# A graph network kernel: a third pair of banks for the first pass's sums, and one-hots by one wide comparison

## The reference

```python
# layer 0: attention by a scalar score per edge
logits = leaky(h_trans[src] @ a_src + h_trans[dst] @ a_dst); exp_l = exp(logits)
alpha = exp_l / (segment_sum(exp_l, dst)[dst] + 1e-09)
h_neigh = segment_sum(alpha * (x @ W1.T + b)[src], dst)
# layer 1: four heads, weights from Q[dst] * K[src]; agg = segment_sum(weighted V[src], dst)
# layer 2: e = silu(silu(cat(h[row], h[col]) @ We1 + be1) @ We2 + be2); agg = segment_sum(e, row)   # the edge MLP
# layer 3: two graph convolutions, out = segment_sum(h[row] * norm, col)
```

## Time and profile before

| | |
|---|---|
| median of 3 runs | 6950.0 us (6945.59 to 6977.82) |
| span of the profiled execution | 5685.5 us, 82572 instructions |
| around the span (median less span) | 1264.5 us |
| busy in the span: POOL | 3958.0 us, 70% |
| DVE | 3263.6 us, 57% |
| PE | 3113.8 us, 55% |
| ACT | 1491.5 us, 26% |

### The profile page before, as it was taken

How to read it: one execution, slowest core, us unless ns; L and a number is a source line. 1 busy time by engine, 2 the same in 40 slices (tenths; PEclk the granted TensorE clock), 3 DMA queues, 4 the chain that set the end, 5 groups by cost and what they waited for, 6 DMA issues and landing times. The chain is left out here.

```text
span 5685.5 us, 82572 instructions
## 1 busy us (share of the span) xinstructions
PE 3113.8 (55%) x17051; PEld 2734.5 (48%) x17052; DVE 3263.6 (57%) x12090; ACT 1491.5 (26%) x5626; POOL 3958.0 (70%) x4054
## 2 busy tenths in 40 slices
PE   4444444356666666778898988433333443333333
PEld 3333333345555555657777776333333343333332
DVE  6888887676787787744444444433444443344445
ACT  2333333345555555532222223100000000000001
POOL 3777777736777777367777772677777757777774
PEclk7555555568888777865555556666666666666666
DMA  5111112214444444222121110111111121111112
GB/s 123 52 52 52 52 52 56 49 52 131 132 132 131 130 131 131 70 54 56 52 56 51 53 52 21 56 52 51 51 51 51 51 61 52 51 51 51 51 51 57
DMA packets 222234, 385.68 MB, mean 68 GB/s; under 512 B 85452, under 2 KB 121882, under 8 KB 221998
## 3 DMA queue, kind: packets, MB, share of 16 engines
q0 software_dynamic: 142944, 296.35, 19.0%
q1 hardware_dynamic: 79054, 86.72, 5.0%
HBM read 356.23 MB, written 26.56 MB: 67 GB/s over the span
## 5 line engine op out<-in xcount | busy, mean ns | idle before, releaser
L2246 POOL DMA_INDIRECT arena<-table_gcn,idx_now x1568 | 1532.2, 977 | 642.9 <-issue 422.1
L2296 PE MATMUL pair<-arena,hotf 128*128 x3328 | 726.6, 408 | 1224.7 <-POOLq L1819 1199.3
L2296 PEld LDWEIGHTS pair<-arena,hotf 128*128 128x128 f32 x3328 | 691.2, 317 | 1256.1 <-issue 1255.8
L664 POOL DMA_INDIRECT arena<-table_attention,idx_now x832 | 825.7, 992 | 272.7 <-issue 197.2
L664 POOL DMA_INDIRECT arena<-table_key_value,idx_now x832 | 789.2, 949 | 275.9 <-issue 221.1
L1852 POOL DMA_INDIRECT arena<-table_edge_mlp,idx_now x784 | 768.1, 980 | 261.2 <-issue 212.4
L2323 DVE TENSOR_TENSOR acc<-acc,pair 128x1024 f32 x208 | 253.9, 1221 | 1133.9 <-PE pair L2299 1133.9
L1069 PE MATMUL pair<-wide,hotf 128*128 128x130 f32 x1664 | 431.0, 439 | 653.3 <-ACT wide L1033 653.3
L1069 PEld LDWEIGHTS pair<-wide,hotf 128*128 128x128 f32 x1664 | 369.0, 326 | 718.5 <-ACT wide L1033 718.5
L2256 ACT COPY idx_now<-src_t 128x8 int32 (+1 forms) x204 | 39.3, 197 | 1815.2 <-PE pair L2299 1803.2
L1406 PE MATMUL pair<-wide,hotf 128*128 128x132 f32 x1664 | 314.1, 347 | 232.9 <-DVE acc L1436 232.8
(11 more groups left out here) (371 smaller groups left out, 5709.7 us busy)
## 6 DMA issues: line engine op xcount, KB each, us to landing
key<-rel_dram SPq DMA_DIRECT2D x104, 256.0 KB, 3.4
arena<-rel_dram SPq DMA_DIRECT2D x52, 512.0 KB, 3.7
arena<-table_gcn,idx_now POOLq DMA_INDIRECT x1568, 2.5
arena<-table_attention,idx_now POOLq DMA_INDIRECT x832
arena<-table_key_value,idx_now POOLq DMA_INDIRECT x832
arena<-table_edge_mlp,idx_now POOLq DMA_INDIRECT x784, 2.4
table_attention<-arena SPq DMA_DIRECT2D x13, 512.0 KB, 3.0
table_gcn<-acc SPq DMA_DIRECT2D x26, 256.0 KB, 2.3
```

The source lines that it names most:

```text
L664: q_.indirect_dma_start(ring[:, slot, 0:width], None, table, bass.IndirectOffsetOnAxis(ap=idx_now[:, slot:slot + 1].bitcast(U32), axis=0)) ...
L2246: q_.indirect_dma_start(conv_ring[:, slot * D:(slot + 1) * D], None, table, bass.IndirectOffsetOnAxis(ap=idx_now[:, slot:slot + 1].bitcast ...
L2296: t_.matmul(window[:, bass.ds(offset * D, D)], hot8[:, g % 2, u, :], conv_ring[:, bass.ds(slot * D, D)], start=False, stop=False)
```

## The change

The first pass gets a third pair of banks for its sums (`l0_bank`: pairs 0, 1 and 3 of PSUM in turn, one bank of a pair for each two steps). Additions are made three groups later instead of two. PE waits for the group three before. A product of the sort that used pair 3 goes to pair 2. The four one-hots of a group are made by one `tensor_tensor` of 128x512 (`hots`, which exists already), and in the edge MLP the eight of a group by one of 128x1024; both compare `iota`, repeated, with `rel_now`, repeated. `rows_of` gets a second register and an operation that bounds the loaded value from below.

```diff
--- before.py
+++ after.py
@@ -735,6 +735,10 @@
         rel_out = junk[:, 1, :].bitcast(BF16)[:, 0:COLS]
         turned, late, decoded = [], {}, []
         LOOKED_UP = (ITERS - 3) * RING
+
+        def l0_bank(k, u):
+
+            return pair[(0, 1, 3)[k % 3]][:, u // 2 * 512 + u % 2 * AW:u // 2 * 512 + u % 2 * AW + D + 2]
 
         def unrolled(step):
 
@@ -865,7 +869,7 @@
                     dve.wait_ge(sort_lastB, 1)
                     ch(v.scalar_tensor_tensor(out=key[:, :].rearrange("q (b p) -> q b p", **by_block),
                                               in0=iota[:, :].unsqueeze(1).to_broadcast([P, SORT // P, P]), scalar=float(SORT // P),
-                                              in1=pair[3][:, :].rearrange("q (b p) -> q b p", **by_block), op0=ALU.mult, op1=ALU.add))
+                                              in1=pair[2][:, :].rearrange("q (b p) -> q b p", **by_block), op0=ALU.mult, op1=ALU.add))
                     counts, e, node, base = (tiny[:, n, :] for n in range(4))
                     for b in range(SB):
                         yield
@@ -927,12 +931,10 @@
 
                     k = i * RING + g
                     ch = Chain(dve, l0_v, 2 * k)
-                    add = back(*later(i, g, -2)) if past >= 2 else lambda u: None
+                    add = back(*later(i, g, -3)) if past >= 3 else lambda u: None
                     nodes = nodes_of(dve, regs, g)
                     dve.wait_ge(l0_placed, k + 1)
-                    for u in range(G):
-                        v.tensor_scalar(out=hotf[:, g, u, :], in0=iota[:, :], scalar1=rel_now[:, g * G + u:g * G + u + 1], scalar2=None,
-                                        op0=ALU.is_equal)
+                    v.tensor_tensor(out=hotf[:, g, :, :], **hots(g))
                     add(0)
                     for u in range(G):
                         last = v.scalar_tensor_tensor(out=junk[:, 0, u * P:(u + 1) * P], in0=iota[:, :],
@@ -962,7 +964,7 @@
                         else:
                             dve.wait_ge(l0_sum, k + 1)
                             dve.wait_ge(l0_acc[G - 1], k + 2)
-                        v.tensor_add(here, here, bank[2 * (g % 2) + u // 2][:, (u % 2) * AW:(u % 2) * AW + D + 2]).then_inc(l0_acc[u], 1)
+                        v.tensor_add(here, here, l0_bank(k, u)).then_inc(l0_acc[u], 1)
                     return add
 
                 def step_and_load(i, g, past, left):
@@ -977,7 +979,7 @@
                 dve.sem_inc(l0_acc[G - 1], 2)
                 load_nodes(dve, regs, 0, 0)
                 unrolled(step_and_load)
-                for g in range(RING - 2, RING):
+                for g in range(RING - 3, RING):
                     add = back(ITERS - 1, g)
                     for u in range(G):
                         add(u)
@@ -1058,16 +1060,15 @@
                     pe.wait_ge(pick_made, 1)
                     pe.wait_ge(sort_last, 1)
                     for h in range(2):
-                        last = t_.matmul(bank[6 + h], pick_last[:, :], last_tile[:, h * 512:(h + 1) * 512], start=True, stop=True)
+                        last = t_.matmul(bank[4 + h], pick_last[:, :], last_tile[:, h * 512:(h + 1) * 512], start=True, stop=True)
                     last.then_inc(sort_lastB, 1)
 
                 def step(i, g, past, left):
                     k = i * RING + g
                     pe.wait_ge(l0_wide, k + 1)
-                    pe.wait_ge(l0_acc[G - 1], k + 1)
+                    pe.wait_ge(l0_acc[G - 1], k)
                     for u in range(G):
-                        last = t_.matmul(bank[2 * (g % 2) + u // 2][:, (u % 2) * AW:(u % 2) * AW + D + 2],
-                                         hotf[:, g, u, :], wide[:, g, u, 0:D + 2], start=True, stop=True)
+                        last = t_.matmul(l0_bank(k, u), hotf[:, g, u, :], wide[:, g, u, 0:D + 2], start=True, stop=True)
                     last.then_inc(l0_sum, 1)
                     if k in turns:
                         turn(*turns[k])
@@ -1822,8 +1823,10 @@
 
         def rows_of(eng, need, table, k):
 
-            eng.reg_load([need], table[0:1, bass.ds(k, 1)])
-            return eng.snap(need, min_val=0, max_val=CTILE_GROUPS - 1) + 1
+            loaded, bounded = need
+            eng.reg_load([loaded], table[0:1, bass.ds(k, 1)])
+            eng.reg_alu(bounded, loaded, 0, ALU.max)
+            return eng.snap(bounded, min_val=0, max_val=CTILE_GROUPS - 1) + 1
 
         def at_least(eng, signal, k, more):
 
@@ -1973,7 +1976,7 @@
             def _(dve):
                 first = [dve.alloc_register(f"l2_node{g}") for g in range(2)]
                 slots = [dve.alloc_register(f"l2_slot{u}") for u in range(CG)]
-                need = dve.alloc_register("l2_need")
+                need = [dve.alloc_register(f"l2_need{n}") for n in range(2)]
 
                 def hot_look(i, g, k):
                     dve.wait_ge(l2_rel_in[g % 4 // 2], 16 * (k // 4 + 1) if isinstance(k, int) else 4 * k - 4 * (g % 4) + 16)
@@ -1994,10 +1997,8 @@
                 def hot_sum(k, g):
                     dve.wait_ge(l2_placed, from_group(k, LAG))
                     at_least(dve, l2_sum, k, -1)
-                    for u in range(CG):
-                        last = v.tensor_scalar(out=hot8[:, g % 2, u, :], in0=iota[:, :], scalar1=rel_now[:, g * CG + u:g * CG + u + 1], scalar2=None,
-                                               op0=ALU.is_equal)
-                    last.then_inc(l2_same, 1)
+                    v.tensor_tensor(out=hot8[:, g % 2, :, :], in0=iota[:, :].unsqueeze(1).to_broadcast([P, CG, P]),
+                                    in1=rel_now[:, g * CG:(g + 1) * CG].unsqueeze(2).to_broadcast([P, CG, P]), op=ALU.is_equal).then_inc(l2_same, 1)
 
                 def add(k, g):
                     dve.reg_load([first[g % 2]], step2_node[0:1, bass.ds(k * CG, 1)])
@@ -2279,7 +2280,7 @@
                 def _(pe):
                     slots = [pe.alloc_register(f"{name}_slot{u}") for u in range(CG)]
                     offsets = [pe.alloc_register(f"{name}_offset{u}") for u in range(CG)]
-                    need = pe.alloc_register(f"{name}_need")
+                    need = [pe.alloc_register(f"{name}_need{n}") for n in range(2)]
 
                     def step(i, g, k):
                         window = pair[g % 3]
```

## The result

The changed kernel takes 6875.28 us (median of 6871.84 to 6899.6), the kernel before 6947.8 us beside it (6940.91 to 6977.82): ratio 0.9887, 95% interval 0.9864 to 0.991. It is 1.1% faster, some 75 us; 6945 was forecast, and the range ended at 6905.

What follows compares the result with a forecast made beforehand. POOL's gathers were taken to set the pace in the first and third passes. Holds of gathers, -7 and +2 us, gave -5 with all else zero, so 6950 - 5 = 6945 us; range 6905 to 6988.

Steps and rivals of the forecast that it cites:

- POOL sets the pace: First and third passes: POOL's gathers, 1.32 and 1.28 us each, bound the kernel; DVE's work costs nothing as such.
- DVE waits for a landing either way, so this is hidden by POOL's pace, and is worth zero directly: Wide one-hots: DVE time 0.17 us sooner per first-pass group, 0.43 per edge-MLP group, priced at zero.
- The time around the span: 1264.5 us around the profiled 5685.5 us span: taken as unchanged, with 16 us less by instruction count kept for the low end.
- Third pair, later additions, `rows_of`: zero: First-pass sums and the waits' register operations: DVE waited only 2.19 us for PE's sums, so no gain; `rows_of` zero too.
- Holds: Gathers starting inside a DVE operation with both inputs in SBUF wait what is left less 0.13 us; together -5 us.
- my limit of 0.06: A gather is held only if the DVE operation began at least 0.06 to 0.1 us before it.
- I summed +2: Edge MLP, change in holds: 12.4 + 5.5 - 4.8 - 17 + 6 = +2 us.
- I summed -7: First pass, change in holds: 9.9 new, -0.9 behind line 934, -4 behind line 938, -12 at line 759: -7 us.
- 12.4 + 5.5: Edge MLP, new holds by the wide comparison: 12.4 us over 28 bursts, 5.5 as half for 11 more at the edge.
- were to lose 12: First pass, line 759: half of its 24.2 us of holds was taken to go as gathers shift, -12 us.
- The locking rival: Gathers repeatedly caught by the wide comparison; half of the edge-MLP groups give 53 us, so 7000 us; chance 0.12.
- The rival that the short comparisons were the blockers: All 40 us of first-pass holds and 4.8 in the edge MLP go with the short one-hots: 6905 us; chance 0.03.

Runs made afterwards that it cites:

- e1_regs: The kernel before with the changed `rows_of` alone: 7064.23 us, ratio 1.0008 to the kernel before.
- e2_banks: The kernel before with the changed `rows_of`, third pair of banks and additions three groups later, short one-hots kept: 7050.58 us, ratio 0.999 to the kernel before.
- e4_mlpwide: The kernel before with the changed `rows_of` and the edge MLP's one-hots by one wide comparison: 7036.54 us, ratio 0.996 to the kernel before.
- e3_p1wide: The kernel before with the changed `rows_of` and the first pass's one-hots by one wide comparison: 7022.3 us, ratio 0.9958 to the kernel before.
- e9_sem3: The changed kernel with three semaphore steps more on VectorE's sequencer in each first-pass group: 6899.86 us, ratio 0.9913 to the kernel before.
- e11_work: The changed kernel with one 128x256 comparison more on VectorE in each first-pass group: 6908.44 us, ratio 0.9921 to the kernel before.
- e8_reduce: The changed kernel with the first pass's four fused comparisons not accumulating and one sum behind them: 6866.9 us, ratio 0.9873 to the kernel before.
- e10_sem9: The changed kernel with nine semaphore steps more on VectorE's sequencer in each first-pass group: 6943.65 us, ratio 0.9971 to the kernel before.
- e7_pad_act: The changed kernel with small ScalarE copies added, three per first-pass group and seven per edge-MLP group: 6886.62 us, ratio 0.9905 to the kernel before.

## Why the prediction was wrong, point by point

**POOL sets the pace (failed for the launches that are timed).** It held for the execution of rows 1 to 10. In timed launches GpSimd runs dry behind VectorE and TensorE, for 293.3 us at one line in the first pass.

**"DVE waits for a landing either way, so this is hidden by POOL's pace, and is worth zero directly" (the step that failed).** It is worth 46.6 us in the first pass by the stretches, some 35 in the whole time, and 22 to 34 in the third. In the first pass, by the prices found above, 37 of the 46 are the 624 instructions that fall and 8 the shorter computing. The wait for a landing that was to hide it, 205.9 us in the earlier trace rows, is 7.5 us in e1_regs. Why the third pass gains stays open.

**The time around the span (the step behind it).** "I take zero and keep 16 for the low end" treated 1264.5 us as lying outside. It is inside, as stalls between instructions: the first pass of the kernel before takes 1363.7 us in e1_regs and 1096.9 in the earlier trace rows. All by count gave 16 us since it spread the time evenly over all 82572 instructions. VectorE's in the first pass cost 0.060 us each, four times the 0.015 of that mean.

**Third pair, later additions, `rows_of`: zero.** Right, within the intervals: 0.999 (0.998 to 1.0) for the three and 1.0008 for `rows_of`. The reason given, 2.19 us of waiting for TensorE's sums, was read from the execution of rows 1 to 10; in e1_regs it is 13 us, and e2_banks gained 0.1%, the end of its interval being 1.0.

**Holds.** The rule, what is left less 0.13 us, was right; the limit at the start and the sum were not. A gather in the profile after, third pass:

```profile
4107.86 1.21 DVE L2000 TENSOR_TENSOR hotf<-iota,rel_now 128x1024 f32<-128x1024 f32 x1
4107.90 1.99 POOL L1855 DMA_INDIRECT arena<-table_edge_mlp,idx_now  x1 [0.30 <-issue]
```

It starts 0.04 us into the comparison, has 1.17 left, and by the rule is held 1.04: 0.944 + 1.04 = 1.98, measured 1.99. Its start at 0.04 would have been free by my limit of 0.06. Third-pass gathers of e1_regs and of e4_mlpwide:

```profile
L1854 POOL DMA_INDIRECT arena<-table_edge_mlp,idx_now x784 | 754.8, 963 | 568.6 <-ACT rel_now L1880 350.6 <-issue 217.7 <-DMA arena<-table_edge_mlp,idx_now 0.3
```

```profile
L1854 POOL DMA_INDIRECT arena<-table_edge_mlp,idx_now x784 | 806.2, 1028 | 483.3 <-ACT rel_now L1880 257.7 <-issue 224.7 <-DMA arena<-table_edge_mlp,idx_now 0.9
```

+51 us of GpSimd's time where I summed +2, and +26 in the first pass (windows of e1 and e3) where I summed -7. Followed gather by gather, the trace of e4_mlpwide has 72 that start within the wide comparison and are held over 0.03 us, 52.3 us together, where 12.4 + 5.5 was summed. In e3_p1wide the wide comparison holds 28, 9.4 us, as summed (9.9); the sum fails at line 759, whose holds went up from 17.9 us in e1_regs to 32.7 and were to lose 12. The locking rival's size of holds came out (53 us), whether distances repeat as it said wasn't looked at, and its time was wrong: GpSimd had idle time to take the holds (568.6 us before, 483.3 after). The rival that the short comparisons were the blockers names a time of 6905 for a reason that isn't there, since holds rose.

**What was to be seen.** The first pass's mean is 1014 ns against 975 to 1000, the third's 1009 against 965 to 1000. The median is 944, as said. "DVE's idle time before line 948 up by 35 us" can't be read from rows 1 to 10 either: it is 161.5 us after, 206.6 there and 102.5 in e1_regs. Nor can "the second pass and the last two within 5 us of now". In launches on one chip the second pass, which no run touched, differs by up to 19 us (1391.2 in e9_sem3, 1372.0 in e11_work), the last two by under 7 where they weren't touched. The first-pass gathers end 202 us later than in rows 1, which I had named as a sign of error, and it was one of the reading and not of the change.

## What to carry to other kernels

Before a span is subtracted from a median, look whether that execution is one of those that are timed: a span 18% under the time, as here, meant that the recorded execution lacked the stalls of the timed ones, and its rows had no word of them. Where rows show "issue" idle inside a busy engine, or gaps that don't end on its data, price an edit by instructions as well as by work: in the first pass here some 0.060 us for each VectorE instruction and only 0.17 us for a us of computing (estimates), though GpSimd is the busiest engine of the span (59%, VectorE 47%). Trading four instructions for one may pay even at more computing: e8_reduce, with 118 us more of it, is the fastest run here (0.9873), though its interval does not part it from the changed kernel (0.9893).

## What the runs showed of the hardware

In timed launches an engine passes stretches in which instructions go 0.70 us or a multiple of it apart, some 8 us long on VectorE in the first pass, about one in 25 us. One lasts about what 128 instructions cost, 128 x 0.060 = 7.7 us. The packets of one instruction queue (q14, 1.25 MB in 153, 8 KB each) go roughly with VectorE's count: 153 in e1_regs, 148 in e3_p1wide (624 fewer instructions, 4.9 times 128), 140 in the profile after, 162 in e10_sem9 (1872 more than after, 14.6 times 128). e7_pad_act has 148 as well, with small copies on ScalarE, so the queue is not VectorE's alone. In e1_regs packets of q14 start at VectorE's records 1600, 1728, 1857, 1985, 2117 and 2241, so about every 128. This looks like the supply of instructions, block by block.

But the blocks alone are not what costs. The execution of rows 1 to 10 has the same 82572 instructions, its q14 packets start at the same six records, and it has no such stretch. Nor are the packets slower where the stretches are: those of 8 KB in the first pass take 0.44 us at the median in both. What makes instructions go 0.70 us apart in the timed launches was not shown, nor that the stretches are waits for instructions at all.

The Trainium skill, page "Runtime: NRT & Kernel Launch", section "Instruction fetch mechanics", says that instructions are refilled in blocks of 16 KiB, 256 instructions, and that crossing a block is mostly hidden. Packets of 16 KB are on another queue here (q8, 1.36 MB in 83); those that come every 128 records of VectorE have 8 KB, half of what the page says. That crossing is hidden agrees with the execution of rows 1 to 10, which has no stretch. In the timed launches something that goes with the count of instructions is not hidden: 46.6 us in one pass from 624 fewer.
